# Equal contiguous halves of an image, fp32 leftovers in layer 1, shorter statistics chains and new engine orders in a group-norm, Hadamard and three-layer token network

## The reference, cut to what matters

```python
# x: (16, 192, 56, 56) fp32; 3136 tokens an image, 192 channels a token
x = x + hadamard(_gn(x))              # y = token[192] @ H[192 x 192] / 16
x = x + net(_gn(x))
def _gn(v, G=32, eps=1e-5):           # mean and variance over 6 channels x 3136 tokens
    ...
def net(t):                           # for each token
    h = gelu(layernorm(t @ W1.T + b1) * g1 + beta1)
    h = gelu(layernorm(h @ W2.T + b2) * g2 + beta2)
    return h @ W3.T + b3
```

## Time and profile before

| | |
|---|---|
| median of 3 runs | 940.06 us (938.57 to 940.89) |
| profiled execution: its own time | 939.64 us |
| profiled execution: span from first to last instruction | 937.9 us |
| granted TensorE clock over the span | 0.979 |
| HBM read, written | 40.45 MB, 38.54 MB |
| instructions | 22620 |

### The profile page before, as it was taken

How to read it: one execution, slowest core, us unless ns; L and a number is a source line. 1 busy time by engine, 2 the same in 40 slices (tenths; PEclk the granted TensorE clock), 3 DMA queues, 4 the chain that set the end, 5 groups by cost and what they waited for, 6 DMA issues and landing times.

```text
span 937.9 us, 22620 instructions
## 1 busy us (share of the span) xinstructions
PE 850.5 (91%) x8521; PEld 559.6 (60%) x8521; DVE 859.1 (92%) x1508; ACT 809.4 (86%) x2348; POOL 570.3 (61%) x413
## 2 busy tenths in 40 slices
PE   0558999999999999999999999999999989989897
PEld 0125666666666666666666666666666556656663
DVE  5999999999999999999999999999999989876466
ACT  1946898999989898989989898989989888978983
POOL 0314576666766666766757666766756666657660
PEclk9877999999999999999999999999999999999999
DMA  9451042242332242332332332332321111121213
GB/s 258 133 139 33 2 126 82 82 124 71 102 97 76 86 121 68 105 102 71 110 96 69 95 112 68 105 102 71 105 82 56 57 46 35 35 68 36 68 35 102
DMA packets 49020, 80.45 MB, mean 86 GB/s; under 512 B 11536, under 2 KB 11664, under 8 KB 48784
## 3 DMA queue, kind: packets, MB, share of 16 engines
q1 hardware_dynamic: 48912, 79.01, 27.9%
HBM read 40.45 MB, written 38.54 MB: 84 GB/s over the span
## 4 chain that ended last, share of the span: by engine, by line
PE 45%; DVE 41%; ACT 6%; POOL 4%; issue 2%; SPq 1%; DMA 1%; ACTq 0%; DVEq 0%
PE tm L534 11%; DVE z L1317 8%; PE tp L546 5%; PE tm L529 5%; PE hl L443 5%; DVE bn L1158 4%; DVE X L1133 4%; DVE xs_lo L1109 3%; PE hl L381 3%; PE hl L448 3%; DVE xs_lo L1113 3%; PE tp L553 2%; DVE x_lo L1296 2%; PE tm L523 2%; DVE bn L1089 2%; POOL ge_lo L957 2%
## 5 line engine op out<-in xcount | busy, mean ns | idle before, releaser
L957 POOL TENSOR_TENSOR ge_lo<-ge,ge_hi 128x512 f16<-128x512 f32 (+1 forms) x190 | 329.9, 1748 | 88.7 <-ACT ge_hi L749 88.7
L949 POOL TENSOR_TENSOR rs<-ssq,neg_half 128x4 f32<-128x4 f32 x196 | 212.5, 1084 | 178.2 <-ACT z L719 176.8
L719 ACT ACTIVATE z<-tm 128x194 f32<-128x194 f32 x784 | 249.7, 332 | 31.4 <-PE tm L534 25.6
L1317 DVE TENSOR_TENSOR z<-tm,rs 128x768 f32<-128x768 f32 x196 | 185.8, 948 | 31.0 <-POOL rs L949 30.4
L731 ACT ACTIVATE ge<-tp,par 128x512 f32<-128x512 f32 x196 | 153.5, 783 | 41.7 <-PE tp L546 40.9
L719 ACT ACTIVATION_READ_ACCUMULATOR z<-tm 128x1 f32 x784 | 163.7, 209 | 0.1
L749 ACT ACTIVATE ge_hi<-ge 128x512 f16<-128x512 f32 (+1 forms) x190 | 159.8, 848 | 4.3
L546 PE MATMUL tp<-cst,z 128*128 128x128 f32 x784 | 124.2, 281 | 18.9 <-DVE z L1317 17.8
L546 PEld LDWEIGHTS tp<-cst,z 128*128 128x128 f32 x784 | 85.6, 143 | 44.7 <-DVE z L1317 35.3
L534 PE MATMUL tm<-w_hi,ge_hi 128*128 128x192 f16 x392 | 98.0, 250 | 0.0
L1158 DVE BATCH_NORM_STATS2 bn<-X 128x6 f32<-128x512 f32 x144 | 96.6, 682 | 0.5
(11 more groups left out here) (198 smaller groups left out, 2109.4 us busy)
## 6 DMA issues: line engine op xcount, KB each, us to landing
X<-x SPq DMA_DIRECT2D x48, 512.0 KB, 4.0
out<-X SPq DMA_DIRECT2D x48, 512.0 KB, 2.9
X<-x SPq DMA_DIRECT2D x96, 128.0 KB, 4.1
out<-X SPq DMA_DIRECT2D x96, 128.0 KB, 3.0
X<-weights SPq DMA_DIRECT2D x1, 1024.0 KB, 11.6
XL<-x SPq DMA_DIRECT2D x16, 32.0 KB, 3.4
out<-left SPq DMA_DIRECT2D x2, 256.0 KB, 3.1
cst<-consts SPq DMA_DIRECT2D x1, 320.0 KB, 5.9
```

The source lines that it names most:

```text
L719: last = nc.scalar.activation(z[n][:, 2 * h + k, i * TW:(i + 1) * TW], tm[h][:, i, k * TW:(k + 1) * TW], ACT.Square, scale=float(C) ** -0. ...
L949: nc.gpsimd.tensor_tensor(rs[n][:, 2 * h:2 * h + 2, :], ssq[n][:, 2 * h:2 * h + 2, :], neg_half[0:TT, 0:4].rearrange("p (i k) -> p i k", i=2),
L957: nc.gpsimd.tensor_tensor(ge_lo[n][:, g % 2, PART[h], :], ge[n][:, PART[h], :], ge_hi[n][:, g % 2, PART[h], :], ALU.subtract).then_inc(s_g ...
L1317: nc.vector.tensor_tensor(z[n][:, 2 * h:2 * h + 2, 0:2 * C].rearrange("p k (i o) -> p i k o", i=2), tm[h][:, :, 0:2 * TW].rearrange("p i ( ...
```

## The change

- **Halves.** `SIDE = HW // 2` = 1568 tokens, so the halves are the two contiguous halves of the image and both have 3 x 512 + 32 tokens. The leftover is 32 tokens of each half (`REM = 32`), stored as 96 columns on all 128 partitions: 32 + 32 of blocks 0 and 1, and 32 of block 2. `side` goes.
- **DMA.** A leftover is loaded by three DMAs of 128-byte rows instead of two of 256-byte rows. The leftovers of all images are stored by four DMAs in both kernels, now with 128-byte rows, twice as many rows.
- **Chains.** One aggregation of block 2 instead of two; one subtraction of the bias (a tensor_tensor); mean*mean is one tensor_tensor and its addition to the variance another; the weighting by token count goes (a factor 0.5 in the constants).
- **Leftover in layer 1.** ACT scales it to fp32 (`left1_ab`, `left1_c`), no lo part is made, and PE multiplies it in fp32 by `w32`. `h_left` is 14 matmuls of 32 columns instead of 8 of 64.
- **Semaphore.** The lo part of unit 2 (made on POOL) has its own semaphore `s_first_lo`.
- **Orders.** New lists on all engines.

```diff
-SIDE = U * UT
-REM = HW - 2 * SIDE
+SIDE = HW // 2
+DONE = U * UT
+REM = SIDE - DONE
...
 # gn_stats
-                        for i in range(2):
-                            rows = slice(64 * i, 64 * i + 64)
-                            last = nc.vector.bn_aggr(gst[rows, 1, :, n], bn[n][rows, q % 2, 2 * U + 1:3 * U + 1 + (i == side(q)[0]), :]
-                                                     .rearrange("p u s -> p (u s)"))
+                        last = nc.vector.bn_aggr(gst[:, 1, :, n], bn[n][:, q % 2, 2 * U + 1:3 * U + 2, :].rearrange("p u s -> p (u s)"))
...
-                        for k in range(2):
-                            last = nc.vector.tensor_scalar(gst[:, k, 0, 1:2], gst[:, k, 0, 1:2], b3[:, k:k + 1], None, ALU.subtract)
-                        mark(last)
+                        mark(nc.vector.tensor_tensor(gst[:, :, 0, 1], gst[:, :, 0, 1], b3, ALU.subtract))
                 elif stage == 2:
                     joined()
-                    for k in range(2)[ks]:
-                        for n, q in images:
-                            mean = gst[:, k, 0, n:n + 1]
-                            last = nc.vector.tensor_scalar(gst[:, k, 1, n:n + 1], mean, mean, gst[:, k, 1, n:n + 1], ALU.mult, ALU.add)
-                    mark(last)
+                    mark(nc.vector.tensor_tensor(gsq_ch[:, ks, ns], gst[:, ks, 0, ns], gst[:, ks, 0, ns], ALU.mult))
...
-                    if len({q // 8 for n, q in images}) == 1:
-                        half = images[0][1] // 8
-                        last = nc.vector.tensor_scalar(gst[:, 1, :, ns], gst[:, 1, :, ns], lower_share[:, half:half + 1], None, ALU.mult)
...
+                    nc.vector.tensor_tensor(gst[:, ks, 1, ns], gst[:, ks, 1, ns], gsq_ch[:, ks, ns], ALU.add).then_inc(s_gst, 1)
...
-            def split_left_lo(g):
-                for q in LEFT_AT.get(g, ()):
...
 # PE, group: the leftover unit in layer 1
-                terms = ((hi, w_hi[n]), (hi, w_lo[n]), (lo, w_hi[n]))
+                if n == 0 and g == DPOS:
+                    terms = ((None, w32),)
+                else:
+                    terms = ((hi, w_hi[n]), (hi, w_lo[n]), (lo, w_hi[n]))
...
 # ACT, step
             def step(g):
+                scaled_hi(h_unit(g + 1), 0)
+                squares(g, 0, 0, 0)
                 scaled_left_hi(h_unit(g + 1))
-                squares(g, 0, 0, 0)
-                split_left(g)
-                scaled_hi(h_unit(g + 1), 0)
                 squares(g, 0, 0, 1)
                 gelu(g - 2, 1, 1)
...
+                split_x1(unit_at(g + 1), 0)
                 scaled_hi(h_unit(g + 1), 2)
-                split_x1(unit_at(g + 1), 0)
+                squares(g - 1, 1, 0, 0)
+                split_x1(unit_at(g + 1), 2)
                 gelu(g, 0, 0)
-                split_x1(unit_at(g + 1), 2)
-                squares(g - 1, 1, 0, 0)
                 squares(g - 1, 1, 0, 1)
...
 # ACT, step_norm: the end of the list
                 split_x1(unit_at(g + 1), 2)
                 squares(g - 1, 1, 1, 0)
                 gelu(g, 0, 1)
                 squares(g - 1, 1, 1, 1)
+                gelu_hi(g, 0, 1)
                 gelu(g - 1, 1, 0)
                 gelu_hi(g - 1, 1, 0)
-                gelu_hi(g, 0, 1)
...
 # ACT, last
                 squares(g - 1, 1, 1, 0)
+                gelu(g, 0, 1)
                 squares(g - 1, 1, 1, 1)
-                gelu(g, 0, 1)
                 gelu_hi(g, 0, 1)
...
 # DVE, step
                 stats_x1(h_unit(g), 0)
+                residual(h_unit(g), 2)
                 stats_part(g, 2)
-                residual(h_unit(g), 2)
                 scaled_lo(h_unit(g + 1), 0)
```

More of the change, by code:

```diff
@@ L414, in h_left @@
                 pe.wait_ge(s_xsl_lo, q + 1)
-                free("a")
-                i = side(q)[0]
-                parts = xsl_hi[:, i], xsl_lo[:, i]
-                for k, terms in enumerate(((AA, CA_), (AC_, CCD))):
-                    for b, m in enumerate(terms):
-                        for r, part in enumerate(parts):
-                            last = nc.tensor.matmul(hl[:, 0, k * REM:(k + 1) * REM], h16[:, m, :], part[:, b, :],
-                                                    start=(k == 0 and b == 0 and r == 0), stop=(b == 1 and r == 1),
-                                                    skip_group_check=True)
+                free("a", "b")
+                parts = xsl_hi, xsl_lo
+                lower = hl[:, 0, REM:2 * REM]
+                for i in range(2):
+                    for r, part in enumerate(parts):
+                        nc.tensor.matmul(hl[:, i, 0:REM], h16[:, AA, :], part[:, i * REM:(i + 1) * REM], start=(r == 0), stop=False,
+                                         skip_group_check=True)
+                for r, part in enumerate(parts):
+                    nc.tensor.matmul(lower, h16[:, CCB, :], part[:, 2 * REM:3 * REM], start=False, stop=False, skip_group_check=True)
+                for r, part in enumerate(parts):
+                    for i in range(2):
+                        rows = slice(64 * i, 64 * i + 64)
+                        nc.tensor.matmul(hl[:, i, 0:REM], h16[rows, CA_, :], part[rows, 2 * REM:3 * REM], start=False,
+                                         stop=(r == 1), skip_group_check=True)
+                for r, part in enumerate(parts):
+                    for i in range(2):
+                        cols = slice(64 * i, 64 * i + 64)
+                        last = nc.tensor.matmul(lower[cols], h16[:, AC_, cols], part[:, i * REM:(i + 1) * REM], start=False,
+                                                stop=(r == 1), skip_group_check=True)
                 last.then_inc(s_h_left, 1)
-                held["a"] = s_res_left, q + 1
+                held["a"] = held["b"] = s_res_left, q + 1
             def l3_ab(g):
@@ L560, in step @@
                 group(g, 0, 0)
-                h_left(h_unit(g))
                 transposes(g - 2, 1, 1)
@@ L566, in step @@
                 h_c(h_unit(g))
+                w1_shift(chain_at(g))
                 group(g - 1, 1, 0)
@@ L573, in step @@
                 transposes(g - 1, 1, 0)
-                w1_shift(chain_at(g))
+                h_left(h_unit(g))
                 h_shift(chain_at(g))
             def step_left(g):
-                gn_means(chain_at(g))
                 group(g, 0, 0)
                 transposes(g - 2, 1, 1)
+                gn_means(chain_at(g))
                 h_ab(h_unit(g))
@@ L593, in step_left @@
                 transposes(g - 1, 1, 0)
+                h_shift(chain_at(g))
             def step_norm(g):
@@ L845, in drain @@
                 squares(g, 0, 0, 0)
+                gelu_hi(g, 0, 0)
+                split_x1(unit_at(g + 1), 0)
                 squares(g, 0, 0, 1)
@@ L852, in drain @@
                 gelu(g, 0, 0)
-                split_x1(unit_at(g + 1), 2)
-                gelu_hi(g, 0, 0)
+                gelu_hi(g, 0, 1)
                 squares(g - 1, 1, 0, 0)
@@ L877, in moments @@
                         act.wait_ge(s_load[a], 48)
-                    act.wait_ge(s_load_left[1], 32)
+                    act.wait_ge(s_load_left[1], 48)
                 flat = (ge_hi[1], ge_lo[0])[part][:, :, :, :].rearrange("p a b t -> p (a b t)")
-                rest = ge_lo[1][:, part, 0, 0:REM]
+                rest = ge_lo[1][:, part, 0, 0:2 * REM]
                 scale = float(HW) ** (-1, -0.5)[part]
@@ L921, in _ @@
             centre(0)
+            centre(1)
             scaled_hi(U, 0)
-            centre(1)
             scaled_hi(U, 2)
@@ L1120, in scaled_left_lo @@
                 dve.wait_ge(s_xsl_hi, 2 * (q + 1))
[L1121 to L1125 removed]
+                for k, cols in ((0, slice(0, 2 * REM)), (1, slice(2 * REM, 3 * REM))):
+                    last = nc.vector.scalar_tensor_tensor(out=xsl_lo[:, cols], in0=XL[:, q % RL, cols], scalar=scale1(q, k),
+                                                          in1=xsl_hi[:, cols], op0=ALU.mult, op1=ALU.subtract)
+                last.then_inc(s_xsl_lo, 1)
             def residual(a, b):
```

291 lines of the change are left out of this document (139 added, 152 removed).

## The result

The changed kernel takes 991.11 us (median of 4 runs, 987.09 to 996.19), the kernel before 940.47 beside it: a ratio of 1.0551, 95% interval 1.0522 to 1.0579. It is slower by 51 us where 18 less were forecast, and lies outside the range. The four runs of the changed kernel spread over 9.1 us, and the slowest has the lowest granted clock (0.959; 0.968 in the fastest).

A forecast was written before the change was run, and what follows sets the result against it. VectorE was taken to bound the 12 steady images, the loop over the engines the two behind them. 939.64 - 19 + 2.4 + 0.95 + 0.1 - 1.7 - 1.3 + 0.5 = 921.6, forecast 922 us; 915 to 928 (54%), 8 in 10 within 909 to 940.

The forecast's parts named there:

- I price the steady moves at 0: Steady images: the reordered calls on ScalarE and VectorE were taken to cost 0 us.
- The second rival: In `step`, the `xsl_lo` pair falls behind GpSimd in every image, 2.7 us against 1.8 saved: 952 us, 14%.
- VectorE gets earlier, not later: Argument in `step` against the `xsl_lo` pair falling behind GpSimd, a case priced at 952 us.
- I add nothing: Statistics chain: no wait behind GpSimd was priced for the new two-input tensor_tensors, 0 us.
- The alternative sum: Statistics chain: each new triple caught once for 0.86 us, 10 us higher over 12 images, 932 us.
- VectorE's saving: Steady images: fewer chain and leftover instructions on VectorE, 1.8 us an image, 21.7 over 12 images.
- The steady part was to lose 19 us: 12 steady images: of 21.7 us saved on VectorE, 19 shorten the time.
- the cap: Steady part: TensorE's idle time, 19.2 us, limits the gain, perhaps soft by some us.
- the first rival: Steady part: VectorE's saving turns into waits; 941 us with nothing saved, 931.5 with half, centre 937; 17%.
- The start was to lose 1.2: Start: shorter prologue chains, -1.7 us, and more DMA packets for the first images' leftovers, +0.5.
- The leftover unit was to cost +0.95: Leftover unit on TensorE: fp32 matmuls in place of fp16 ones, +0.95 us for both halves, bounds -1.0 to +4.9.
- `last` was to cost 2.4: ScalarE's list in `last`: a 0.64 us pair of squares before `gelu_hi`, four steps, +2.4 us, bounds 0 to 2.8.

The follow-up runs named there:

- e11: Changed kernel with ScalarE's old list in `step` alone; 948.9 us.
- e13: Changed kernel with one call moved in ScalarE's `step`: `gelu(g, 0, 0)` back two calls, near its old place; 937.9 us.
- e14: Changed kernel with only the first calls of ScalarE's `step` in the old order, `gelu(g, 0, 0)` staying late; 947.7 us.
- e1: Changed kernel with the old lists and prologues on ScalarE and VectorE, new data and tensor_tensors kept; 941.6 us.
- e7: Changed kernel with the old lists on ScalarE and VectorE and all small chain instructions in one-input form; 922.46 us, ratio 0.982.
- e5: Changed kernel with mean*mean + variance made by the old one-input instructions, all else as changed; 966.3 us.
- e10: Changed kernel with one-input chain, `xsl_lo`, `normalise(g - 1, 1, 0)` and `stats_x1(.., 1)` earlier on VectorE, ScalarE's old `last`; 911.04 us, ratio 0.9695.
- e2: The kernel before, old data and starts, with the new lists of the steps on ScalarE and VectorE; 975.1 us.
- e12: Changed kernel with one-input chain instructions, `xsl_lo` ahead of `normalise(g, 0, 1)` in VectorE's `step`, and ScalarE's old `last`; 917.4 us.
- e9: e7 with `stats_x1(.., 1)` moved ahead of `scaled_lo(.., 2)` in VectorE's `step_left`; 924.8 us.

## Why the prediction was wrong

**The step that failed** is "I price the steady moves at 0", with its ground that only ScalarE's and VectorE's calls are real and the transposes hide them. The calls were read rightly, and ScalarE's transposes were not the danger. What I did not follow is the next engine: ScalarE's order sets the start of GpSimd's `rs` and with it of `ge_lo`, and that start stands in a race with VectorE's two-input instructions. The price is 41.3 us of the 50.4 (e11, e13, e14). The second rival had the mechanism, its place (the `xsl_lo` pair in `step`) and nearly its price, 2.7 us (measured 2.8 for the pair); it was short of the trigger, `x_lo`'s 0.98 ahead of it, and had 14%. "Against: VectorE gets earlier, not later" was the wrong argument: it is later within the step once it has lost one tie. Its 952 us was short because it priced the pair alone, without `x_lo`, the chain's stall and the clock. With margins of 0.54 us in the earlier trace rows and 0.28 at `x_lo` and an order rewritten on the engine that feeds the other party, the honest chance was near even.

**"I add nothing" for the new tensor_tensors** failed too. One of each triple stands in every steady image of e1 and of after: 1.8 us each, 14.8 us of the steady part with the old orders (e1 against e7: 633.9 and 619.1), 22.7 with the new ones (after against e5), the lower clock that comes with them included. The Trainium skill's rule (SBUF — State Buffer, "Who interferes with whom") is what the runs show: the instruction issued second waits for the whole of the first. I set it aside because of the earlier trace rows, a one-input instruction that stood. That row is 128x2; of the seven that the change removed six are 128x1, which do not stand (e7's rows above), and the seventh is the earlier trace rows's own line, L1207. No row stood for the two-input form that came. The alternative sum that I wrote beside it, one triple caught once an image for 10 us, was the right reading and 5 us low. (In the working on `xs_lo`, 303.44 + 1.64 = 305.08 is 0.55 us behind 304.53, not 0.66; the 0.9 us of stall are read from the durations and stand.)

**The terms of the sum.** e7 has the whole change but the orders and the two-input form, so it is the sum without `last`: 921.6 - 2.4 = 919.2 for a measured 922.5. It agrees within 3.3 us, but by two errors that mostly cancel, those of the steady part and of the start:

- VectorE's saving was 1.8 us an image; measured in e7 (621.5 - 602.1) / 12 = 1.6, with the squares in their old form. Right.
- The steady part was to lose 19 us, up to TensorE's idle time. It lost 10.6, and TensorE is still idle for 9.1. So the cap was not TensorE's work: the first rival, saving that turns into waits, held for about half (8.8 us more idle time on VectorE). e10 reaches 15.0 with another order.
- The start was to lose 1.2 (1.7 less, 0.5 more for the DMAs). It ends at 103.8 to 107.9 us over the 14 new-data kernels, for 110.3 before and 110.5 in e2 with the old data: 2.4 to 6.5 less. It belongs to the data part; which piece of it was not tried.
- The leftover unit was to cost +0.95. From its first matmul's start to its last one's it is 5.30 us for 4.03, +1.27. Its fp32 records show 340 and 329 ns, as the earlier trace rows had it.
- `last` was to cost 2.4 with bounds of 0 and 2.8; it costs 4.3. The bound failed since the cost is not the 0.64 us of squares on ScalarE, four times, but one caught `bias` on VectorE and the lower clock behind it (e12, e13). The working also took in one of the list's two moved pairs of squares.

```profile
L553 PE MATMUL tm<-w,left_ab 128*128 128x192 f32 x16 | 3.1, 340 | 0.0
L548 PE MATMUL tm<-w,left_c 64*128 64x192 f32 x16 | 1.7, 329 | 0.0
```

**TensorE's clock had no term.** The prediction took the steady part at the full level, as in the kernel before. The account of the 50.4 us, by runs: 41.3 for the caught course of `x_lo` and `xsl_lo` (12 x 3.44, seven images with lower clock in either course); 19.7 for `gsq_ch` and what comes with it (638.8 against 619.1, another order in between), of which 7 x 1.6 = 11.2 are the lower clock and 12 x 0.71 = 8.5 the rest; less 10.6 gained. The sum is 50.4 by its making, since 638.8 is the steady part of e13 and 629.7 - 10.6 = 619.1 that of e7.

What stays open: why the image that has lost the tie comes back to it to within 0.02 us each time (the starts differ by 0.01 to 0.03 us in twelve images) where e2 leaves it after six, and whether another small shift would have reached the bad course with the old lists.

## What to carry to other kernels

Where VectorE instructions with two SBUF inputs run beside GpSimd, every such pair is a race for the whole length of the other's instruction: list for one period each pair with its margin, the ones that are won included (a GpSimd instruction longer than usual is their sign), and treat any change of order on an engine that feeds either of them as a change of those margins. Small instructions in such a kernel are best kept in a form that does not take part (here one element a partition with scalars from memory), even if that is more of them: four that run free take 0.95 us, one that is caught 1.98. And when a change carries data and orders, measure them apart: here the data part is worth -18 us with one-input chains (e7) and nothing with tensor_tensors (e1), the new orders +50 on top of the latter (after against e1), and with a third order and one-input chains the whole is -29 (e10). Before a loss is put down to stalls alone, look at the granted clock: here more than a fifth of it came that way.

## What the runs showed of the hardware

- Starts recorded within 0.03 us of each other don't tell who wins. `x_lo`, recorded 0.01 to 0.03 us ahead of `ge_lo`, stood in all 18 cases (12 images of after, 6 of e2; 2.25 to 2.28 us for 1.27). The chain's subtraction, recorded up to 0.015 us behind the start of a `ge_lo`, ran free in all steady images of after (0.15 us), and 0.21 behind it stood in all of e1 (1.94). From 0.28 us ahead `x_lo` won, and GpSimd stood (1.99 to 2.02 for 1.16).
- VectorE instructions with one SBUF input differ by their width. After the first 100 us of the 16 traces, 577 of one column in the chain began inside a running `ge_lo` with more than 0.15 us of it left, and none took longer than usual; of 2 or 4 columns 35 did so (`gst`, `gvar`, `gshift`), and all 35 took longer, up to 1.46 us for 0.23 (e2, 101.1 us). The Trainium skill (VectorE: DVE Perf Modes, "Mode 2×_2P — use both read ports for one tensor") says that a one-source instruction in SBUF can take both read ports where its outermost dimension longer than one is even, or odd and equal in source and destination, which fits; no run here varied the width alone.
- TensorE's granted clock over the steady part was 0.98 of 2.4 GHz after and 1.00 before and in e7, e9 and e10. The 0.98 is seven stretches at 1.2 GHz behind waits of TensorE, and its busy time there is 624.4 us for the 610.0 of e7, with the same 6328 matmuls.
